# Destination tiles padded to groups of 32 edge records instead of blocks of 128: a list of superblock-and-tile units steers the sums

## The chip, the cores and the metric

The kernel runs on one core of one Trainium2 chip. The metric is the device time of one execution in microseconds (us). The core has five engines with their own instruction streams: PE (TensorE, matrix products), DVE (VectorE), ACT (ScalarE), POOL (GpSimd, which issues the indirect DMAs here) and SP (SyncE, which issues plain DMAs). They wait for each other on semaphores only.

## The reference

A graph layer over 3125 nodes of 256 channels, with 50,000 edges, in this form:

```python
xn = layernorm(x)
x = x + gnn(xn, src, dst, edge_weight) + mix(xn)
x = x + moe_ffn(layernorm(x))          # top 2 of 8 experts

def gnn(x, row, col, val, W, b):       # row = src, col = dst
    support = segment_sum(val[:, None] * x[col], row, num_segments=3125)
    return relu(concatenate([x, support], axis=1) @ W + b)
```

`mix` is a chain of pointwise convolutions with a batch norm, a linear attention inside groups of 32 channels and a residual map. All of it is in float32. The change concerns `support`: for every edge a row is fetched by `dst`, weighted and added to the row of `src`. The kernel fetches rows of the product with the second half of W (`y_d`), so that the sums land directly on the layer's output.

## The kernel before, in words

**Tiles and blocks.** The 3125 nodes are 25 tiles of 125 rows (`NT`, `T`). At run time the edges are sorted by the tile of their `src` into records of index, row within the tile and weight (three bf16 parts). The sort works in groups of 32 records (`GE`). Each tile's groups are padded up to whole blocks of 128 records (`nblk`, `bcum` of line 1122 on, with `EG` = 4 groups a block), so a block belongs to one tile. The list is as long as it can ever need to be: `EB` = 415 blocks.

**Work of a block.** POOL gathers 128 rows of 256 channels into a ring of 15 slots (lines 518 to 524). DVE compares the row numbers of 8 blocks at once with an iota (`hots`, line 1210). ACT scales one block's 0/1 matrix by the weights (`select`, line 874), up to 8 ahead. PE multiplies it with the gathered rows (`sum_edges`, line 641); a float32 product shows as two MATMUL records. Two blocks share a PSUM bank (`pair`, line 316), two banks alternate. DVE adds each block's 125 x 256 sum to its tile in `ACC` (`add_sums`, line 1233). Which tile that is comes out of a packed row: four 5-bit digits per loaded word (`digits`, line 1224). PE may be two banks, that is four blocks, ahead of DVE (`need(pe, g_acc, b - 2)`).

**Stages.** The order of every engine is written out by hand. After the sort come: the projection, 42 products of 500 columns (`project`, line 651) with 2 blocks each; the batch norm, with 18 blocks; the mixing stage, 28 segments of one tile each (`SEG`, line 697 on for PE, 1311 on for DVE), with 281 blocks dealt out in quarters of a segment (`mark`, `cut4`); a closing part with the last 32 blocks (`GT`) between 25 column operations of DVE and 25 squares of ACT, and then between 25 additions to `X`. Then the router, and a loop over 56 blocks of tokens for the experts.

**Within a segment** DVE does `shrink` and `key_sums`, a quarter of the additions, `inverses` (a reciprocal of 125 x 512, line 1292), a quarter, `values` and `queries`, a quarter, `products`, a quarter. PE does `channel_rows`, a quarter of the blocks, `channel_sums`, a quarter, `mix_transpose`, a quarter, `mix_out`, a quarter.

**Loads.** SP loads three experts' W2 (1 MB each) during the closing part, each behind a count of finished additions (line 420), and all of W1 once PE has done the last block.

## Time and profile before

| quantity | value |
|---|---|
| device time, three runs | 1198.22, 1188.03, 1197.9 us; median 1197.9 |
| profiled execution, span from first to last instruction | 1198.5 us |
| busy share of the span | PE 83%, weight loads 67%, DVE 63%, ACT 49%, POOL 54% |
| gathers | 415, the first at 155.83 us, the last at 702.0 us |
| mean granted clock of TensorE | 0.889 of full speed |
| HBM traffic | 86.44 MB read, 18.42 MB written |

The profile is of one execution. Its span, 1198.5 us, is all that the page gives of that execution's own time; it is 0.6 us above the median of the three runs. Busy time says how long an engine was at work, not whether somebody waited for it: for that one reads what ended the idle time before an instruction, and in the chain of waits which work was late.

### The profile page before, as it was taken

The page shows a single profiled execution, that of the slowest core. Times are in us where ns is not written, and L with a number is a line of the kernel's source. Part 1 is how long each engine was busy: PE and PEld are TensorE (multiplying, and loading weights), DVE is VectorE, ACT ScalarE, POOL GpSimd, SP SyncE. Part 2 cuts the span into 40 slices and gives each one's busy share as a digit, 9 for nine tenths or more (in the row PEclk, how much of TensorE's full clock was granted, in tenths as well). Part 3 has the DMA queues.
Part 4 walks back from the last instruction along what each step waited for, and adds up shares of the span by engine and source line. Part 5 has one row for each costly group of instructions (what it writes and reads, how often), then busy time and mean ns, then how long its engine had stood idle before and what let it go on. Part 6 is the DMA issues. An engine that isn't in the chain of part 4 may idle for free.

```text
span 1198.5 us, 20145 instructions
## 1 busy us (share of the span) xinstructions
PE 992.0 (83%) x5428; PEld 804.2 (67%) x5429; DVE 757.2 (63%) x1675; ACT 587.7 (49%) x1528; POOL 650.2 (54%) x620
## 2 busy tenths in 40 slices
PE   2779879985787777787777777499999999999995
PEld 1346545553566656666665457389999999999995
DVE  8999866653777777777877895634444444444441
ACT  0445445559766777766766733233333333333331
POOL 4393367777777777766767761214333344333332
PEclk8899989996878888888988765599999999999998
DMA  7012133333333333333333559352222222222221
GB/s 169 27 36 86 37 90 105 104 104 105 103 101 103 104 103 104 100 95 90 100 93 98 157 214 361 112 162 37 39 41 36 36 36 36 37 39 38 38 37 18
DMA packets 55071, 105.72 MB, mean 88 GB/s; under 512 B 15337, under 2 KB 37070, under 8 KB 52822
## 3 DMA queue, kind: packets, MB, share of 16 engines
q0 software_dynamic: 31312, 70.22, 23.8%
q1 hardware_dynamic: 23075, 33.81, 9.0%
q10 hardware_dynamic: 611, 0.87, 0.2%
q8 instruction: 28, 0.46, 0.2%
q14 instruction: 45, 0.37, 0.1%
HBM read 86.44 MB, written 18.42 MB: 87 GB/s over the span
## 4 chain that ended last, share of the span: by engine, by line
PE 54%; DVE 24%; issue 12%; DMA 3%; DVEq 3%; SPq 1%; ACT 1%; POOL 1%; ACTq 0%; POOLq 0%
PE ps L778 15%; PE ps L788 15%; PE ps L646 8%; DVE arena_c L1242 7%; PE ps L693 5%; PE ps L655 5%; DVE arena_a L1175 3%; DVE arena_a L1169 2%; DVE arena_c L1292 2%; DMA arena_c<-y_d,arena_e 1%; PE ps L724 1%; DVEq L1230 1%; PE ps L768 1%; SPq L450 1%; PE ps L735 1%
## 5 line engine op out<-in xcount | busy, mean ns | idle before, releaser
L523 POOL DMA_INDIRECT arena_c<-y_d,arena_e x415 | 407.9, 983 | 146.3 <-issue 87.4
L646 PE MATMUL ps<-arena_c,arena_e 128*125 128x256 f32 x830 | 257.7, 434 | 111.6 <-DVE arena_c L1242 97.0
L646 PEld LDWEIGHTS ps<-arena_c,arena_e 128*125 128x125 f32 x830 | 161.2, 213 | 190.1 <-issue 151.7
L1242 DVE TENSOR_TENSOR arena_c<-arena_c,ps 125x256 f32 x415 | 172.5, 416 | 100.3 <-PE ps L646 85.0
L555 POOL DMA_INDIRECT out<-node,bn x56 | 99.4, 1776 | 250.2 <-DVE node L1526 225.8
L879 ACT ACTIVATE arena_e<-arena_e 128x125 f32<-128x125 bf16 x415 | 190.6, 508 | 69.9 <-PE ps L646 57.4
L1002 ACT ACTIVATE arena_d<-ps,small 128x128 f32<-128x128 f32 x448 | 121.9, 383 | 181.0 <-PE ps L778 142.9
L788 PE MATMUL ps<-arena_c,arena_d 128*128 x896 | 204.0, 381 | 0.5 <-issue 0.5
L788 PEld LDWEIGHTS ps<-arena_c,arena_d 128*128 128x128 f32 x896 | 167.0, 191 | 21.4 <-issue 0.7
L778 PEld LDWEIGHTS ps<-node,arena_d 128*128 128x128 f32 x896 | 105.8, 194 | 2.6 <-DVE node L1518 1.2
L778 PE MATMUL ps<-node,arena_d 128*128 128x128 f32 x896 | 106.1, 277 | 0.8 <-DVE node L1518 0.8
L778 PEld LDWEIGHTS ps<-node,arena_e 128*128 128x128 f32 x896 | 104.4, 192 | 2.4 <-DVE node L1518 1.1
L778 PE MATMUL ps<-node,arena_e 128*128 128x128 f32 x896 | 104.7, 275 | 0.8 <-DVE node L1518 0.8
L1531 DVE TENSOR_SCALAR arena_e<-arena_e 128x256 f32<-128x256 f32 x56 | 23.1, 413 | 113.4 <-DMA arena_e<-z_d,bn 113.4
L1292 DVE RECIPROCAL arena_c<-arena_c 125x512 f32<-125x512 f32 x25 | 83.7, 3347 | 4.4 <-issue 4.4
L693 PE MATMUL ps<-arena_d 128*125 128x256 f32 x200 | 73.5, 534 | 0.0
L655 PE MATMUL ps<-arena_c,arena_d 128*128 128x500 f32 (+1 forms) x168 | 71.5, 549 | 2.3 <-DVEq L1208 2.3
L544 POOL DMA_INDIRECT arena_e<-z_d,bn x56 | 56.0, 1000 | 25.5 <-issue 12.8
L1013 ACT ACTIVATE node<-ps,bn 128x256 f32<-128x256 f32 x56 | 26.6, 475 | 86.0 <-PE ps L788 84.6
L1526 DVE SCALAR_TENSOR_TENSOR node<-arena_a,bn,node 128x256 f32<-128x256 f32 x56 | 27.1, 484 | 61.3 <-ACT node L1013 58.5
L693 PEld LDWEIGHTS ps<-arena_d 128*125 128x125 f32 x200 | 54.5, 272 | 13.1
L1518 DVE TENSOR_SCALAR node<-ps,small 128x128 f32<-128x128 f32 x112 | 40.8, 406 | 27.5 <-PE ps L768 25.9
(315 smaller groups left out, 1361.2 us busy)
## 6 DMA issues: line engine op xcount, KB each, us to landing
arena_c<-in_W SPq DMA_DIRECT2D x8, 1024.0 KB, 6.6
arena_a<-in_W SPq DMA_DIRECT2D x8, 1024.0 KB, 12.1
arena_c<-y_d,arena_e POOLq DMA_INDIRECT x415, 2.8
x<-in_x SPq DMA_DIRECT2D x5, 560.0 KB
z_d<-x SPq DMA_DIRECT2D x5, 560.0 KB
out<-x SPq DMA_DIRECT2D x5, 560.0 KB
y_d<-arena_c SPq DMA_DIRECT2D x15, 125.0 KB
y_d<-arena_a SPq DMA_DIRECT2D x10, 125.0 KB
```

The costliest lines, as they stand in the source:

```text
L523: pool.indirect_dma_start(ring[:, b % GR, :], None, io["y_d"], bass.IndirectOffsetOnAxis(gix[:, b:b + 1], 0)).then_inc(gth[b % GR], 16)
L544: pool.indirect_dma_start(xsb[b % 4], None, io["z_d"], bass.IndirectOffsetOnAxis(fetch[:, b:b + 1], 0)).then_inc(xs_in[b % 4], 16)
L555: pool.indirect_dma_start(io["out"], bass.IndirectOffsetOnAxis(home[:, b:b + 1], 0), ysb[b % 2], None, compute_op=ALU.add, oob_is_err=True ...
L646: nc.tensor.matmul(pair(b), sel[b % SR], ring[:, b % GR, :], start=True, stop=True).then_inc(g_mm, 1)
L655: mm = nc.tensor.matmul(ps[:, j, 0:w], wq[:, k, 128 * j:128 * j + 128], HT[:, k, i * TC:i * TC + w], start=(k == 0), stop=(k == 1))
L693: mm = nc.tensor.matmul(ps[0:T, 5, 0:C], oT[t % 2][:, k, :], wres[:, k, :], start=(k == 0), stop=(k == 3))
L778: mm = nc.tensor.matmul(psf[:, 1024 * s + 128 * j:1024 * s + 128 * j + 128], W1b[s][:, k, 128 * j:128 * j + 128], xeT[s][:, k, :], start=( ...
L788: mm = nc.tensor.matmul(out, gel[s][:, 128 * k:128 * k + 128], W2[:, ds(e, 1), k, :], start=(k == 0), stop=(k == 7))
L879: nc.scalar.activation(sel[b % SR], hot[b // 8 % 2][:, :, b % 8], ACT.Copy, scale=wcols[:, b:b + 1]).then_inc(selm, 1)
L1002: ins = nc.scalar.activation(gel[s % 2][:, 128 * j:128 * j + 128], psf[:, 1024 * (s % 2) + 128 * j:1024 * (s % 2) + 128 * j + 128], ACT.Ge ...
L1242: V.tensor_tensor(part, part, pair(b), ALU.add).then_inc(g_acc, 1)
L1292: V.reciprocal(rden, den[t % 2]).then_inc(v_at, 1)
```

## The change

Tiles are padded to groups of 32 only. Blocks of 128 records (`BG` = 4 groups) now follow each other without regard to tiles: `EB` = 397. Two blocks make a superblock of 256 records (`EG` = 8 groups, `SB` = 199). A unit is the part of one superblock that belongs to one tile; there are at most `EU` = 199 + 24 = 223. Each unit takes two products, one for each block of its superblock, summed in one PSUM bank, and one addition of DVE. Two selection matrices go with each unit (`EN` = 446); records of another tile get a row number outside 0 to 124 and so a zero column. The lists of units (tile, superblock, last unit of each superblock) are computed at run time by `unit_steps` and `unit_rows` on DVE with three small products on PE. PE reads the superblock from a packed row, three to a word. The ring has 16 slots. SP, which was idle then, waits for the two gathers of each superblock and raises `landed`, and waits for the superblock's last unit and raises `freed`, for which POOL waits. Stages: 42 units in the projection, 9 in the batch norm, 156 in the 28 segments, 16 in the closing part (6, 1, 6 and 3). The W2 loads of the closing part go to ACT's queue, between its squares.

```diff
-EB = (EC * T + NT * 127) // 128
+GM = (EC * T + NT * (GE - 1)) // GE
+EB = -(-GM // BG)
+SB = -(-GM // EG)
+EU = SB + NT - 1
+EN = 2 * EU
...
-        def pair(b):
-            return ps[0:T, 6 + b // 2 % 2, C * (b % 2):C * (b % 2) + C]
+        def unit_sums(u):
+            return ps[0:T, 6 + u % 2, 0:C]
...
-            for e in range(3):
-                sp.wait_ge(g_acc, EB - GT + 3 + 8 * e)
-                load_w2(e)
+            for s in range(SB):
+                d = s - (RS - RL)
+                if d >= 0:
+                    if d % 3 == 0:
+                        packed = sp.value_load(nrow[0:1, d // 3:d // 3 + 1], min_val=0, max_val=2 ** 24 - 1)
+                        for i in range(3):
+                            left[d + i] = (packed >> 8 * i) & 255
+                    sp.wait_ge(g_mm, sp.compute_val(left.pop(d) + 1))
+                    sp.sem_inc(freed, 1)
+                for b in range(2 * s, min(2 * s + 2, EB)):
+                    sp.wait_ge(gth[b % GR], 16 * (b // GR + 1))
+                sp.sem_inc(landed, 1)
...
             for b in range(EB):
-                need(pool, g_mm, b - GR + 1)
+                if b % 2 == 0:
+                    need(pool, freed, b // 2 - RS + 1)
...
-            def sum_edges(b):
-                pe.wait_ge(gth[b % GR], 16 * (b // GR + 1))
-                pe.wait_ge(selm, b + 1)
-                if b % 2 == 0:
-                    need(pe, g_acc, b - 2)
-                nc.tensor.matmul(pair(b), sel[b % SR], ring[:, b % GR, :], start=True, stop=True).then_inc(g_mm, 1)
+            def sum_edges(u):
+                if u % 3 == 0:
+                    packed = pe.value_load(srow[0:1, u // 3:u // 3 + 1], min_val=0, max_val=2 ** 24 - 1)
+                    for i in range(3):
+                        blocks[u + i] = pe.compute_val((packed >> 8 * i) & 255)
+                s = blocks.pop(u)
...
+                pe.wait_ge(landed, pe.compute_val(s + 1))
+                pe.wait_ge(selm, 2 * u + 2)
+                need(pe, g_acc, u - 1)
+                for j in range(2):
+                    mm = nc.tensor.matmul(unit_sums(u), sel[(2 * u + j) % SR], ring[:, ds(at + j, 1), :].rearrange("p a c -> p (a c)"),
+                                          start=(j == 0), stop=(j == 1))
+                mm.then_inc(g_mm, 1)
...
-                if b % 2 == 0:
-                    v.wait_ge(g_mm, min(b + 2, EB))
-                need(v, g_acc, b)
-                V.tensor_tensor(part, part, pair(b), ALU.add).then_inc(g_acc, 1)
-                digits(b + 1)
-                if b % 8 == 3:
-                    hots(b // 8 + 2)
+                v.wait_ge(g_mm, u + 1)
+                need(v, g_acc, u)
+                V.tensor_tensor(part, part, unit_sums(u), ALU.add).then_inc(g_acc, 1)
+                digits(u + 1)
+                if u % 4 == 1:
+                    hots(u // 4 + 2)
...
+                if t % 8 == 3:
+                    act.dma_start(W2[:, t // 8, :, :], io["W2"][t // 8]).then_inc(w2_in, 16)
```

On PE, at the start of the projection, before: `L655` is a projection product, `L646` a block's product, its waits on the instruction itself.

```order
L655 MATMUL ps<-arena_c,arena_d 128x500 [waits acc_ready,ld_w,y_ready,edge_records]
L655 MATMUL ps<-arena_c,arena_d 128x500
L646 MATMUL ps<-arena_c,arena_e 125x256 [waits selection_ready,gathered0]
L646 MATMUL ps<-arena_c,arena_e 125x256 [waits selection_ready,gathered1]
L655 MATMUL ps<-arena_c,arena_d 128x500 x2
L646 MATMUL ps<-arena_c,arena_e 125x256 [waits selection_ready,gathered2]
L646 MATMUL ps<-arena_c,arena_e 125x256 [waits selection_ready,gathered3]
```

The same place in the changed kernel, where `L706` is the projection product and `L685` to `L695` are one unit.

```order
L706 MATMUL ps<-arena_c,arena_d 128x500 [waits ld_w,edge_records]
L706 MATMUL ps<-arena_c,arena_d 128x500
L685 TENSOR_LOAD arena_e
L685 ISA x2
L687 REGISTER_ALU x5
L689 REGISTER_ALU
L689 ISA
L695 ISA [waits selection_ready,superblocks_landed]
L695 MATMUL ps<-arena_c,arena_e 125x256
L695 ISA
L695 MATMUL ps<-arena_c,arena_e 125x256
L706 MATMUL ps<-arena_c,arena_d 128x500 x2
```

Two blocks' products have become two products with four register and address instructions around them, twelve in every third unit, and the wait stands on an instruction of its own ahead of the first product.

On DVE, from one addition of a mixing segment to the next `shrink`, before: `L1242` adds a block, `L1228` and `L1230` unpack digits, `L1214` is `hots`, `L1280` `shrink`.

```order
L1242 TENSOR_TENSOR arena_c<-arena_c,ps 125x256 [waits g_acc]
L1228 TENSOR_LOAD arena_e
L1228 ISA x2
L1230 REGISTER_ALU x7
L1214 TENSOR_TENSOR arena_e<-arena_e,arena_d 128x1000 [waits selection_ready]
L1238 ISA
L1242 TENSOR_TENSOR arena_c<-arena_c,ps 125x256 [waits g_acc,g_mm]
L1238 ISA
L1242 TENSOR_TENSOR arena_c<-arena_c,ps 125x256 [waits g_acc]
L1280 TENSOR_SCALAR small<-small 125x1 [waits mix_root]
```

The same quarter in the changed kernel: `L1319` adds a unit, `L1306` and `L1308` unpack digits, `L1356` is `shrink`.

```order
L1319 TENSOR_TENSOR arena_c<-arena_c,ps 125x256 [waits g_acc,g_mm]
L1306 TENSOR_LOAD arena_e
L1306 ISA x2
L1308 REGISTER_ALU x7
L1316 ISA
L1319 TENSOR_TENSOR arena_c<-arena_c,ps 125x256 [waits g_acc,g_mm]
L1356 TENSOR_SCALAR small<-small 125x1 [waits mix_root]
```

Three additions have become two, each of two blocks. Over the stage it is 281 before and 156 now, and one unpacking goes to four units where it went to four blocks.

On SP, which had nothing here before, early in its loop over superblocks: `L440` loads a packed word, `L443` unpacks it.

```order
L443 REGISTER_ALU x2
L443 REGISTER_ALU [waits g_mm,gathered10,gathered11]
L443 REGISTER_ALU x2
L443 REGISTER_ALU [waits g_mm,gathered12,gathered13]
L443 REGISTER_ALU x2
L440 TENSOR_LOAD arena_e [waits g_mm,gathered14,gathered15]
L440 ISA x2
L443 REGISTER_ALU x2
```

Each wait names the last unit of an old superblock (`g_mm`) and the two gathers of a new one; the following register instructions carry the two signals.

## Rows read from the trace of the kernel before

**Rows 1.** The page: busy time by engine, and the gathers' and selections' groups
```profile
PE 992.0 (83%) x5428; PEld 804.2 (67%) x5429; DVE 757.2 (63%) x1675; ACT 587.7 (49%) x1528; POOL 650.2 (54%) x620
...
L523 POOL DMA_INDIRECT arena_c<-y_d,arena_e x415 | 407.9, 983 | 146.3 <-issue 87.4
...
L879 ACT ACTIVATE arena_e<-arena_e 128x125 f32<-128x125 bf16 x415 | 190.6, 508 | 69.9 <-PE ps L646 57.4
...
arena_c<-y_d,arena_e POOLq DMA_INDIRECT x415, 2.8
```

**Rows 2.** Stages: busy us and (x) count of PE, PEld, DVE, ACT, POOL; clock, DMA
```profile
165.00:265.00 100.00, 96.60 (x318) 57.56 (x318) 63.40 (x137) 53.73 (x119) 75.73 (x79) 1.00 0.36 104
265.00:296.00 31.00, 16.72 (x42) 8.75 (x40) 13.59 (x38) 25.94 (x26) 23.60 (x25) 0.76 0.36 105
296.00:669.00 373.00, 286.86 (x1314) 230.22 (x1314) 276.97 (x465) 255.56 (x611) 274.35 (x282) 0.86 0.34 100
669.00:710.00 41.00, 26.91 (x62) 15.63 (x62) 35.91 (x97) 23.55 (x79) 26.32 (x26) 0.64 0.51 164
800.00:1198.00 398.00, 385.12 (x2630) 362.09 (x2630) 166.12 (x470) 138.82 (x470) 148.25 (x106) 0.98 0.24 36
```

**Rows 3.** Timeline of POOL: start, duration; in brackets its idle time before
```profile
155.83 0.99 POOL L523 DMA_INDIRECT arena_c<-y_d,arena_e  x1 [7.10 <-DVE arena_e L1201]
...
159.90 3.82 POOL L523 DMA_INDIRECT arena_c<-y_d,arena_e  x1 [0.31 <-issue]
...
457.62 1.22 POOL L523 DMA_INDIRECT arena_c<-y_d,arena_e  x1 [0.30 <-PE ps L646]
...
497.44 0.94 POOL L523 DMA_INDIRECT arena_c<-y_d,arena_e  x1 [0.85 <-PE ps L646]
...
702.00 0.95 POOL L523 DMA_INDIRECT arena_c<-y_d,arena_e  x1 [0.30 <-issue]
```

**Rows 4.** The gathers in 155 to 497.4 us: busy us and (x) count
```profile
155.00:497.40 342.40, 260.63 (x264) 0.88 0.35 102
```

**Rows 5.** Groups of the mixing stage, 296 to 669 us
```profile
L523 POOL DMA_INDIRECT arena_c<-y_d,arena_e x282 | 275.7, 978 | 99.0 <-issue 60.9 <-PE ps L646 38.0
L646 PE MATMUL ps<-arena_c,arena_e 128*125 128x256 f32 x564 | 170.0, 424 | 85.7 <-DVE arena_c L1242 82.4 <-ACT arena_e L879 2.8
...
L1242 DVE TENSOR_TENSOR arena_c<-arena_c,ps 125x256 f32 x280 | 115.9, 414 | 65.4 <-PE ps L646 54.8 <-DVE arena_c L1242 4.0
```

**Rows 6.** Timeline of DVE in one mixing segment
```profile
457.34 0.68 DVE L1214 TENSOR_TENSOR arena_e<-arena_e,arena_d 128x1000 bf16<-128x1000 bf16 x1 [0.61 <-issue]
...
460.99 3.35 DVE L1292 RECIPROCAL arena_c<-arena_c 125x512 f32<-125x512 f32 x1 [0.75 <-issue]
464.26 1.34 DVE L1242 TENSOR_TENSOR arena_c<-arena_c,ps 125x256 f32 x3
```

**Rows 7.** Timeline of PE: projection, its end, mixing, expert loop
```profile
186.64 1.84 PE L655 MATMUL ps<-arena_c,arena_d 128*128 128x500 f32 x4
188.31 1.03 PE L646 MATMUL ps<-arena_c,arena_e 128*125 128x256 f32 x4
...
270.64 2.23 PE L646 MATMUL ps<-arena_c,arena_e 128*125 128x256 f32 x4 [0.85 <-DMA arena_c<-y_d,arena_e]
...
296.19 1.64 PE L671 MATMUL ps<-small,arena_a 128*125 128x128 f32 x6 [6.16 <-ACT arena_a L898]
...
465.23 1.19 PE L646 MATMUL ps<-arena_c,arena_e 128*125 128x256 f32 x2 [3.30 <-DVE arena_c L1242]
...
1004.34 0.38 PE L768 MATMUL ps<-small,arena_e 128*128 128x128 f32 x2
1004.56 3.62 PE L788 MATMUL ps<-arena_c,arena_d 128*128 x16
```

**Rows 8.** The chain of waits: DVE's queue just before an addition
```profile
441.62 0.07 DVEq L1238
```

**Rows 9.** Timeline of SP's queue: the issues of W1
```profile
709.50 4.08 SPq L428 DMA_DIRECT2D arena_a<-in_W  x8
```

275 lines of the change are left out of this document (163 added, 112 removed).

## The prediction

> **What bounds the kernel now.** I read the page first. It shows no engine busy throughout, PE 83% and POOL 54% [rows 1], so the share of an average says little and the span has to be cut into stages [rows 2]. The expert loop from 800 us on is PE alone, busy 385 of 398 us, and the change does not reach it. What the change touches lies between the first gather at 155.83 us and the last addition of an edge block, at 710 us.
>
> Next, POOL's timeline [rows 3]. A gather takes 0.94 to 0.95 us with 0.30 between two; 264 have started before the one at 497.44 [rows 4], so the pitch up to there is (497.44 - 155.83) / 264 = 1.294 us. Its wait of 0.85 us for PE is the first that exceeds the usual gap: until then POOL never had to wait for a free slot, after it once in each segment. So POOL paces nothing from the start of the mixing stage on; it only catches up. Had it never waited, 415 gathers at 1.294 us would be through at 693, and the last one starts at 702.0.
>
> In the projection PE is busy 96.6 of 100 us [rows 2]: four records of the projection take 1.67 us from start to start (186.64 to 188.31), and the four of two blocks their 1.03 less an overlap as large as the projection's, 1.84 - 1.67 = 0.17, so 0.86, a period of 2.53 us [rows 7]. Two gathers at 1.294 are 2.59. The two limits are equal there, and at the end of the stage, where the projection products are narrow, PE waits for gathers (0.85 us before 270.64).
>
> In the mixing stage (296 to 669 us, 28 segments, 13.3 us each) nobody is full: PE 287, DVE 277, ACT 256, POOL 274 of 373 us [rows 2]. The groups say who waits for whom [rows 5]: PE waits 82.4 us for additions, and DVE 54.8 us for products. That is a handover chain: DVE is in its reciprocal for 3.35 us, PE has its two banks full and idles 3.30 us (before 465.23), then DVE does three additions in a row [rows 6, 7]. The clock of 0.86 in this stage is the other mark of it, since it falls after such gaps. DVE's own load is higher than its busy time: unpacking digits leaves it idle for 0.61 to 0.75 us a time [rows 6], and each addition has an address instruction of 0.07 us [rows 8], with which I count as much again for the gap around it.
>
> **The sort's end and the start of the projection.** `unit_steps` takes the place of the old block list and is about as long. The weight parts now go through 16 products of 228 columns where 16 transposes of 104 stood, then DVE's four conversions on 456 columns instead of 416. None of this is in my rows; the bounds are 0 and 5 us, and I take 2. The first gather does not wait for it. PE's first products wait for gathers anyway: the fourth, at 159.90, took 3.82 us [rows 3], beside DVE's long bias addition, and this stays. Effect on the end: nothing, because of the gathers; 2 to 5 us if the cover were gone.
>
> **Projection.** 42 units take as long on PE as 84 blocks (four records of 256 columns each), but need 42 x 397 / 223 = 75 gathers instead of 84. PE then no longer waits for them. From the third product, at about 166.5 us (the fourth gather has landed by then), 34 wide periods of 2.53 and 6 narrow ones (125 columns in place of 500, a quarter of 1.67, and 0.86) make 94, so the batch norm starts at about 262 instead of 270. The batch norm is ACT's six activations with 18 selections between them, and keeps its length. The mixing stage starts at 296 - 8 = 288. By then POOL can have done (288 - 155.8) / 1.294 = 102 gathers, and the ring allows 51 x 1.78 + 16 = 107: no stall.
>
> **Mixing, DVE.** A segment has 5.57 units instead of 10.04 blocks. Additions: 4.47 fewer, at 0.414 us [rows 5] and 0.14 for the address [rows 8], 2.5 us. Unpacking: 1.39 instead of 2.51 times, at 0.75, 0.8 us. `hots`: 0.14 more at 0.68, 0.1 us. Net 3.2 us less of 13.3.
>
> **Mixing, PE.** 11.14 products instead of 10.04, that is 2.2 more records at 170.0 / 564 = 0.30 us [rows 5], 0.7 us more; 19 us over the stage. PE's load goes from 287 to 306 us, 10.9 a segment. DVE's was 277 plus what is neither busy nor a wait for products, 373 - 277 - 54.8 = 41, so 318; less 28 x 3.2 = 90 it is 228, 8.1 a segment. Before, the period was 13.3 over a higher load of 318 / 28 = 11.4: a loss of 17% to the handover. The same loss on 10.9 gives 12.7; with no loss it is 10.9.
>
> **Mixing, the register instructions of PE.** A unit has four of them, every third unit a load and seven more. DVE's rows bound the price: 0.75 us for a load with what unpacks it, 0.14 for an address [rows 6, 8]. That is at most 0.75 / 3 + 3 x 0.14 = 0.67 us a unit. From below it is nothing: in the expert loop every product has an address instruction too and 16 records run in 3.62 us right behind L768, without a gap behind a load either [rows 7]. I take 0, as that is the same engine, and the instructions stand behind the previous product and ahead of the wait. The Trainium skill ("Advanced Engine Details and Errata", section Sequencer Loop) says of control instructions that other engine instructions can be read and queued while they execute; PE's expert rows agree, DVE's gaps of 0.61 to 0.75 us do not.
>
> **Mixing, the gathers as a floor.** 368 of 397 gathers must have landed by the end of the stage: 155.8 + 368 x 1.294 + 3.7 = 635.7, which from 288 is 12.4 us a segment. (3.7 us is 0.95 and the 2.8 to landing of [rows 1].) So neither limit gives the full gain of 3.2 us. I take 12.6 us: 28 x 12.6 = 353, the stage ends at 641, and 20 of its 373 us are gone. The gathers' pitch stays: the one at 457.62 takes 1.22 us, 0.27 more, beside a `hots` from 457.34 on, and of those there are 56 instead of 52 [rows 3, 6]; the additions removed read PSUM. The Trainium skill ("SBUF — State Buffer", Who interferes with whom) infers that a `tensor_tensor` leaves descriptor generation alone. By that rule the pitch would be 0.95 + 0.30 = 1.25, 397 gathers 17 us shorter, and the floor would not bind; the row speaks against it.
>
> **ACT** gets 31 more selections of 0.46 us (190.6 / 415) [rows 1], 14 us over 500, and in the mixing stage it idles 117 of 373 us [rows 2]: hidden. Its three W2 issues stand in its loop of squares, which is as long as DVE's there; SP's eight issues of 1 MB take 4.08 us [rows 9], 0.51 each, so 1.5 in sum, and 0 if DVE is later there. **SP's relay** puts a hop between a gather and its product. Even at DVE's 0.75 us it is shorter than the 2.59 of two gathers, so it delays each but slows none, and POOL may be 3 superblocks ahead of SP. I take 0; the other end is 0.75 us once for every stretch in which PE waits for gathers, some 5 in all.
>
> **Closing part**, 41 us before. DVE has 13 additions instead of 25 between its 50 operations: in the first loop ACT's squares hold the time, in the second 6 x 0.41 = 2.4 us go. The rest after the loops is 3 units instead of 7 blocks, 1.5 us. With ACT's 1.5 added back, 38.5 us. The last gather lands at 155.8 + 397 x 1.294 + 3.7 = 673, so it does not hold this part.
>
> **Sum.** 288 + 353 + 38.5 = 679.5 instead of 710, 30.5 us less. Against the profiled span that is 1168.0, and 0.6 less against the median. I say 1168.
>
> **The rivals.**
> - *The handover stays as slow as it is.* PE waits in the reciprocal because two banks are full, and they still are two: PE still gets four products ahead. If each segment keeps 13.3 us, what remains is 8 + 2.5: 1188. For it: the 3.30 us gap is the reciprocal's, not the additions'. Against it: 2.5 us of additions less, and a turn is now one addition.
> - *The gathers alone bind.* With a chain under 12 us the end is 673 + about 3 of last products: 34 us less, 1164. For it speaks DVE's load of 8.1 us; against it the closing part, which follows its own 38.
> - *Slower: PE's register instructions stand on its path.* If a load waits for the array, or the queue is empty after each wait, up to 0.67 us a unit is added: 156 x 0.67 = 105 in the mixing stage, 28 in the projection, 11 in the end. PE's load in mixing would be 306 + 105 = 411; with 20 of waits 431, so 1198.5 + 58 + 28 + 11 - 10.5 = 1285. At half that price it is 378 + waits as before, 1198.5 + 5 + 14 + 5 - 10.5 = 1212. It turns to a loss from some 0.2 us a unit: 306 + 31 = 337, with a tenth of handover 371, and 8 more in the projection. For it: DVE does show such gaps, and in the segments PE, unlike in the expert loop, starts from an empty queue after each wait. Against it: the expert rows.
> - *The change doesn't do what it says:* the counts follow from the constants (397, 446, 223); only a gather count of 415 in the trace would show it. No chance worth a figure.
>
> **How the numbers follow.** The forecast 0.52 (1157 to 1180), the gathers alone 0.10, the unchanged handover 0.25, the register path 0.13. One per cent, 12 us, is about what a measurement of this kernel can tell from no change; the three runs already spread over 10. Faster by over 1% (below 1186): 0.52 + 0.10 + 0.11 of the third case = 0.73. Slower: the register case with 0.12. Within 1%: 0.15. The range 1155 to 1197 holds the first three cases and the unknowns of 5 us at the sort's end; it leaves out the register case and a little on the fast side.
>
> **What would show it.** Right: no PE wait for gathers before 262 us; the mixing stage 345 to 360 us; PE's waits for additions well below 82 us; POOL's waits for a free slot few. Wrong: idle "issue" time of PE ahead of a unit's first product, PE's records of a unit spread over more than 0.9 us in the projection, or segments of 13.3 us with PE idle beside the reciprocal as before.

## The result and the profile after

The changed kernel takes 1161.8 us (median of 4 runs, 1160.4 to 1163.6), the kernel before 1198.1 beside it (4 runs, 1188.0 to 1198.5): a ratio of 0.970, 95% interval 0.966 to 0.975. The forecast was 1168.0 with a range of 1155 to 1197. The profiled execution has a span of 1158.4 us instead of 1198.5, so 40.1 us are to be found in the trace. They stand in two places: 30.1 us up to the last addition of an edge unit, which ends at 679.9 instead of 710.0 us, and 10.0 us behind it (1158.4 - 679.9 = 478.5 instead of 488.5), where the change touches nothing.

The page of the changed kernel, engines, the chain by engine and line, and the groups of the gathers, the units' products, the selections and the additions:

```profile
PE 967.4 (84%) x5493; PEld 789.4 (68%) x5494; DVE 686.8 (59%) x1501; ACT 599.7 (52%) x1559; POOL 635.0 (55%) x603
...
PE 40%; POOL 24%; DVE 12%; DMA 12%; issue 10%; SPq 2%; ACT 0%; DVEq 0%; POOLq 0%; ACTq 0%
...
L550 POOL DMA_INDIRECT arena_c<-y_d,arena_e x397 | 395.6, 996 | 128.2 <-issue 105.7
L695 PE MATMUL ps<-arena_c,arena_e 128*125 x892 | 258.1, 421 | 97.2 <-SPq L447 71.6
...
L929 ACT ACTIVATE arena_e<-arena_e 128x125 f32<-128x125 bf16 x446 | 202.3, 510 | 67.5 <-PE ps L695 53.1
...
L1319 DVE TENSOR_TENSOR arena_c<-arena_c,ps 125x256 f32 x223 | 92.2, 414 | 167.6 <-PE ps L695 164.8
```

The counts are those of the change (397, 446, 223). The two last columns carry the news. TensorE's wait ahead of an edge product now ends with L447, SyncE's relay, which passes on that a superblock's gathers have landed; before, it ended with L1242, the additions [rows 5]. VectorE waits 164.8 us for products: it has become the one with time to spare. And POOL stands in the chain that ended last with 24% of the span.

The stages of the changed kernel by the windows (busy us and count of PE, PEld, DVE, ACT, POOL; granted clock, DMA share, GB/s), cut where [rows 2] cut the kernel before:

```profile
165.00:265.00 100.00, 100.00 (x341) 62.14 (x339) 50.52 (x104) 58.56 (x128) 76.54 (x78) 1.00 0.34 103
265.00:291.00 26.00, 12.83 (x31) 7.83 (x30) 6.91 (x21) 23.92 (x23) 19.60 (x22) 0.63 0.34 103
291.00:643.40 352.40, 278.16 (x1374) 225.02 (x1374) 229.68 (x346) 268.31 (x641) 269.68 (x272) 0.94 0.34 102
643.40:680.00 36.60, 22.48 (x65) 15.02 (x65) 29.85 (x82) 23.08 (x80) 24.34 (x23) 0.81 0.51 170
760.00:1158.00 398.00, 385.16 (x2630) 362.15 (x2630) 164.97 (x469) 138.41 (x470) 147.83 (x106) 0.98 0.23 36
```

The projection has no wait of TensorE's left (100.00 of 100 us). Mixing starts at 291 instead of 296 and takes 352.4 instead of 373 us; the closing part 36.6 instead of 41. The expert loop is the same to 0.04 us.

POOL's timeline, from the first gather to the last:

```profile
158.04 0.99 POOL L550 DMA_INDIRECT arena_c<-y_d,arena_e  x1 [7.53 <-DVE arena_e L1275]
159.33 0.95 POOL L550 DMA_INDIRECT arena_c<-y_d,arena_e  x1 [0.30 <-issue]
...
164.38 3.23 POOL L550 DMA_INDIRECT arena_c<-y_d,arena_e  x1 [0.30 <-issue]
...
460.96 1.41 POOL L550 DMA_INDIRECT arena_c<-y_d,arena_e  x1 [0.30 <-issue]
...
673.30 0.95 POOL L550 DMA_INDIRECT arena_c<-y_d,arena_e  x1 [0.30 <-issue]
```

Between these 397 gathers no idle time is over 0.36 us, so POOL never waits for a free slot: (673.30 - 158.04) / 396 = 1.301 us each, from one end to the other. That is the picture of the rival "the gathers alone bind", not of the forecast, in which gathers and handover were about level. The last gather lands 2.8 us after its start, at 676.1, and the last addition ends at 679.9. What lies between is TensorE's, as its timeline and a window of it show:

```profile
669.21 1.13 PE L695 MATMUL ps<-arena_c,arena_e 128*125 x4 [1.67 <-SPq L447]
671.84 7.59 PE L695 MATMUL ps<-arena_c,arena_e 128*125 x20 [1.50 <-SPq L447]
```

```profile
672.00:678.00 6.00, 6.00 (x15) 4.53 (x16) 4.61 (x12) 0.93 (x2) 1.95 (x2) 0.50 0.21 66
```

At 671.84 TensorE has waited for a gather for the last time. It then works off the last five units in one stretch, most of it at a granted clock of 0.50, to which it has fallen in that wait. So the gathers set the pace up to there, and the last 8 us are products, most of them at the low clock.

The reciprocals of VectorE, one to a mixing segment, show where one limit gives way to the other:

```profile
302.24 3.35 DVE L1368 RECIPROCAL arena_c<-arena_c 125x512 f32<-125x512 f32 x1
...
311.87 3.34 DVE L1368 RECIPROCAL arena_c<-arena_c 125x512 f32<-125x512 f32 x1
...
321.33 3.35 DVE L1368 RECIPROCAL arena_c<-arena_c 125x512 f32<-125x512 f32 x1 [0.74 <-ACT arena_c L975]
...
332.29 3.35 DVE L1368 RECIPROCAL arena_c<-arena_c 125x512 f32<-125x512 f32 x1
```

The first segments take 9.6, 9.5 and 11.0 us. They find some 11 gathered blocks in the ring: at 290.8 us 102 gathers have started and 51 units have used 51 x 1.78 = 91. Once these are used up, from 332.29 on to the 25th reciprocal at 605.70, 21 of them take 13.0 us on average. A segment of 5.57 units needs 5.57 x 397 / 223 = 9.9 gathers, and 9.9 x 1.301 is 12.9. What looked like a stage of even 12.6 us segments, as forecast, is a short fast piece and a long one at the gathers' pace.

The 10 us behind the last addition are in the token products and transposes of the router. Their windows, first of the kernel before (30 us), then of the changed one (18.7 us):

```profile
710.00:740.00 30.00, 29.54 (x150) 28.99 (x150) 17.40 (x62) 10.87 (x27) 13.08 (x16) 0.50 1.00 372
```

```profile
679.90:698.60 18.70, 17.43 (x150) 15.74 (x150) 17.43 (x61) 10.87 (x27) 13.10 (x16) 1.00 0.97 393
```

It is the same work, 150 instructions on TensorE. Before, it runs at a granted clock of 0.50 (1.2 GHz) from end to end, although TensorE is busy 29.54 of 30 us; after, at 1.00 (2.4 GHz). The difference is 11.3 us, of which 10.0 are left at the end of the span.

### The profile page after: what moved, and what is told of

The parts are those of the page before. It is cut to its first block, busy times and chain, and to the rows that moved or that the text cites. A ratio compares the mean times of both kernels' runs of the same rounds, so it can differ in the third digit from the quotient of the medians.

```text
span 1158.4 us, 21890 instructions
## 1 busy us (share of the span) xinstructions
PE 967.4 (84%) x5493; PEld 789.4 (68%) x5494; DVE 686.8 (59%) x1501; ACT 599.7 (52%) x1559; POOL 635.0 (55%) x603
## 4 chain that ended last, share of the span: by engine, by line
PE 40%; POOL 24%; DVE 12%; DMA 12%; issue 10%; SPq 2%; ACT 0%; DVEq 0%; POOLq 0%; ACTq 0%
POOL arena_c L550 24%; PE ps L828 17%; PE ps L838 17%; DMA arena_c<-y_d,arena_e 10%; DVE arena_a L1248 3%; DVE arena_a L1242 2%; SPq L440 1%; PE ps L638 1%; PE ps L818 1%; PE ps L615 1%; PE ps L774 1%; DMA z_d<-gates 1%; DVE small L1109 1%; PE ps L695 1%; DVE arena_a L1245 1%
## 5 line engine op out<-in xcount | busy, mean ns | idle before, releaser
L550 POOL DMA_INDIRECT arena_c<-y_d,arena_e x397 | 395.6, 996 | 128.2 <-issue 105.7
L695 PE MATMUL ps<-arena_c,arena_e 128*125 x892 | 258.1, 421 | 97.2 <-SPq L447 71.6
L695 PEld LDWEIGHTS ps<-arena_c,arena_e 128*125 128x125 f32 x892 | 169.5, 203 | 168.6 <-issue 148.3
L929 ACT ACTIVATE arena_e<-arena_e 128x125 f32<-128x125 bf16 x446 | 202.3, 510 | 67.5 <-PE ps L695 53.1
L1319 DVE TENSOR_TENSOR arena_c<-arena_c,ps 125x256 f32 x223 | 92.2, 414 | 167.6 <-PE ps L695 164.8
L706 PE MATMUL ps<-arena_c,arena_d 128*128 128x500 f32 (+1 forms) x168 | 71.1, 546 | 2.7 <-DVEq L1287 2.7
L571 POOL DMA_INDIRECT arena_e<-z_d,bn x56 | 55.8, 996 | 26.5 <-issue 13.4
L537 POOL DMA_INDIRECT rec_d<-arena_e x20 | 26.4, 1318 | 45.9 <-ACT arena_e L898 45.1
L615 PE MATMUL ps<-node,arena_c 128*125 128x512 f32 x100 | 50.3, 628 | 0.0
## 6 DMA issues: line engine op xcount, KB each, us to landing
arena_a<-in_W SPq DMA_DIRECT2D x8, 1024.0 KB, 12.4
```

The lines of the kernel that those rows point to most:

```text
L550: pool.indirect_dma_start(ring[:, b % GR, :], None, io["y_d"], bass.IndirectOffsetOnAxis(gix[:, at:at + 1], 0)).then_inc(gth[b % GR], 16)
L571: pool.indirect_dma_start(xsb[b % 4], None, io["z_d"], bass.IndirectOffsetOnAxis(fetch[:, b:b + 1], 0)).then_inc(xs_in[b % 4], 16)
L615: mm = nc.tensor.matmul(ps[0:T, 5 + t % 3, :], HT[:, k, T * t:T * t + T], gnn2[:, k, :], start=(k == 0), stop=(k == 1))
L695: mm = nc.tensor.matmul(unit_sums(u), sel[(2 * u + j) % SR], ring[:, ds(at + j, 1), :].rearrange("p a c -> p (a c)"), start=(j == 0), stop ...
L706: mm = nc.tensor.matmul(ps[:, j, 0:w], wq[:, k, 128 * j:128 * j + 128], HT[:, k, i * TC:i * TC + w], start=(k == 0), stop=(k == 1))
L929: nc.scalar.activation(sel[b % SR], hot[b // 8 % 2][:, :, b % 8], ACT.Copy, scale=wcols[:, b:b + 1]).then_inc(selm, 1)
```

## The experiments

All ran beside runs of the kernel before on the same chip. "Mixing segment" is the mean distance of the 25 reciprocals, "last addition" its end in the profiled execution; for the kernel before these are 13.78 us and 710.0, for the changed one 12.64 and 679.9.

**Half of the gathers, in either kernel.** Changed kernel:

```diff
-            for b in range(EB):
-                if b % 2 == 0:
-                    need(pool, freed, b // 2 - RS + 1)
+            for b in range(0, EB, 2):
+                need(pool, freed, b // 2 - RS + 1)
...
-                for b in range(2 * s, min(2 * s + 2, EB)):
+                for b in range(2 * s, 2 * s + 1):
...
-                    ... ring[:, ds(at + j, 1), :] ...
+                    ... ring[:, ds(at, 1), :] ...
```

> The changed kernel with 199 gathers in place of 397: the second gather of each superblock is left out, and both products of a unit read the first one's 128 rows (so half of the edge records contribute nothing, and the others stand in for them). Products, selections and additions keep their number. Theory (in the changed kernel the gathers alone bind the mixing stage, at 1.301 us each without a gap from 158 to 673 us): the segments fall from 12.6 us to what the first of the changed kernel's took while the ring was still full, 9.5 to 11 us, say 10.3; 28 segments make 64 us, so about 1098 us, within 1085 to 1110. Rival (the handover between TensorE and VectorE binds, and the gathers only run beside it): 1162 within 10 us, with segments of 12.6 us as before.

Measured: 1089.3 us (1083.8 to 1093.4), ratio 0.910 (0.903 to 0.917). The segment is 10.13 us, the last addition at 605.8.

The kernel before got the same cut, the product of an odd block reading the slot of the even one:

> The kernel before with every second gather left out (208 in place of 415), the product of an odd block reading the rows of the even one before it. Theory (before the change the handover of additions bound the mixing stage and the gathers only trailed it): segments stay near 13.3 us; POOL's own stretch and the narrow products at the end of the projection give 0 to 10 us, so 1188 to 1198, I say 1193. Rival (before, too, the gathers were what bound): 28 segments go to about 11 us, 60 us less, 1138.

Measured: 1195.9 us (10 runs, 1194.8 to 1198.2), ratio 1.000 (0.997 to 1.003). The segment is 13.74 us, against 13.78 with all gathers. The mixing stage began 5 us earlier, and so did the last addition end, at 705.0.

The same cut takes 73 us from the changed kernel and 2 from the one before. So the gathers bind the one and did not bind the other. The groups say it as plainly. Of the changed kernel with half of its gathers, 300 to 560 us, the window, then additions, gathers, products:

```profile
300.00:560.00 260.00, 233.31 (x1303) 199.23 (x1303) 221.42 (x333) 251.31 (x611) 128.57 (x131) 1.00 0.23 67
...
L1318 DVE TENSOR_TENSOR arena_c<-arena_c,ps 125x256 f32 x146 | 59.6, 408 | 22.2 <-PE ps L694 20.4
L549 POOL DMA_INDIRECT arena_c<-y_d,arena_e x131 | 129.4, 988 | 133.9 <-SPq L444 120.8 <-issue 13.1
L694 PE MATMUL ps<-arena_c,arena_e 128*125 x581 | 147.7, 385 | 26.7 <-DVE arena_c L1318 14.4 <-ACT arena_e L928 11.6 <-SPq L447 0.4
```

And of the kernel before with half of its gathers, the products from 300 to 600 us:

```profile
L647 PE MATMUL ps<-arena_c,arena_e 128*125 128x256 f32 x439 | 134.6, 428 | 72.1 <-DVE arena_c L1243 69.3 <-ACT arena_e L880 2.4
```

In the second, TensorE's 69.3 us of waits for additions stand just as with all the gathers (66.4 us in the same window of the kernel before). In the first, the wait for gathers is 0.4 us, and the next limit comes into sight: ScalarE is busy 251 of 260 us. With its 11 selections and the conversions of a segment it would hold a segment at 251.3 / 260 x 10.13 = 9.8 us, however fast the rest were.

**The register instructions.** As the first, and the superblock of unit u is the constant `u * SB // EU` on TensorE's and SyncE's queues, with no load, unpacking or address instruction:

```diff
-                if u % 3 == 0:
-                    packed = pe.value_load(srow[0:1, u // 3:u // 3 + 1], ...)
...
+                s = u * SB // EU
+                at = s % RS * 2
```

> As the changed kernel with half of its gathers, and besides the list of superblocks is not read: unit u takes superblock u*199//223, a constant, on TensorE's and SyncE's queues, so neither has a load, an unpacking or an address instruction for a unit; the records added are not those of the unit. With the gathers out of the way TensorE's instructions are on the path. Theory (the register instructions of TensorE cost nothing): the same time as with half of the gathers alone, within 5 us. Rival (they stand on TensorE's path at 0.2 us or more a unit): 156 units of mixing at 0.2 to 0.67 us, 30 to 105 us faster than with half of the gathers alone.

Measured: 1081.7 us (1078.6 to 1089.1), against 1089.3 with the gathers alone halved; the intervals of the two ratios (0.899 to 0.913 and 0.903 to 0.917) overlap. The segment is 10.03 instead of 10.13 us, so leaving these instructions out shows in mixing with 0.1 / 5.57 = 0.02 us a unit, 3 us over the stage. ScalarE's 9.8 us stand close under either segment and could hide a little more. The projection is the stricter place, as TensorE has no gap there with half of the gathers. First two periods of the kernel before (no register instructions), then of the changed kernel with them, both with half of the gathers:

```profile
181.88 1.84 PE L656 MATMUL ps<-arena_c,arena_d 128*128 128x500 f32 x4
...
184.42 1.84 PE L656 MATMUL ps<-arena_c,arena_d 128*128 128x500 f32 x4
```

```profile
180.87 1.84 PE L705 MATMUL ps<-arena_c,arena_d 128*128 128x500 f32 x4
...
183.41 1.84 PE L705 MATMUL ps<-arena_c,arena_d 128*128 128x500 f32 x4
```

A period is 2.54 us in both: where TensorE has no gap, these instructions add nothing to the period. The rest of the 12.7 us between the two profiled spans is mostly the router's clock again: behind its last addition the first has 485.5 us left with the token products at clock 0.54, the second 477.0 us with clock 1.00. The rival of 0.2 us a unit or more has fallen.

**Additions twice, in either kernel.** The addition is done once more, into scratch space:

```diff
+                V.tensor_tensor(scratch, part, unit_sums(u), ALU.add)
                 V.tensor_tensor(part, part, unit_sums(u), ALU.add).then_inc(g_acc, 1)
```

> The changed kernel with each unit's addition done twice on VectorE, the first time into scratch space nobody reads: 223 more instructions of 0.41 us. Theory (gathers bind the mixing stage with 2.3 us a segment of slack on VectorE's chain, which is just 5.57 additions of 0.41 us): mixing costs 0 to 10 us more, the closing part 13 additions or 5 us: about 1170, within 1163 to 1180. Rival (the chain through VectorE binds all along): 169 additions after the projection at 0.41 us, 69 us more, 1231.

Measured: 1168.3 us (1162.9 to 1173.5), ratio 0.979 (0.972 to 0.985), so 6.5 us more than the changed kernel; the segment is 12.49 us, not longer than without (12.64).

> The kernel before with each block's addition done twice on VectorE, the first time into scratch space, as it was done to the changed kernel (which it cost 6.5 us): 415 more instructions of 0.41 us, 331 of them after the projection. Theory (before, the chain through VectorE binds): nearly all of the 280 in the mixing stage and of the 50 behind it show, 3.5 us a segment, about 100 us more, 1300, within 1260 to 1330. Rival (VectorE is not on the path before either): up to 20 us more, 1218.

Measured: 1286.6 us (1286.1 to 1287.0), ratio 1.077 (1.070 to 1.085). The segment is 16.72 us, 2.94 more for 10.04 more additions of 0.41 us (4.1): some of it is absorbed, but 88.5 us reach the end. The chain through VectorE's additions was the limit before and no longer is.

**One cut at a time.** In the kernel before, either only the change's number of gathers, or only about its number of additions, or both:

```diff
             for b in range(EB):
+                if b % 23 == 22:
+                    continue
```

```diff
-                nc.tensor.matmul(pair(b), sel[b % SR], ring[:, b % GR, :], start=True, stop=True)...
+                nc.tensor.matmul(pair(b - b % 2), sel[b % SR], ring[:, b % GR, :], start=(b % 2 == 0),
+                                 stop=(b % 2 == 1 or b == EB - 1))...
...
                 if b % 2 == 0:
...
-                V.tensor_tensor(part, part, pair(b), ALU.add).then_inc(g_acc, 1)
+                    V.tensor_tensor(part, part, pair(b), ALU.add).then_inc(g_acc, 2)
```

> The kernel before with the change's number of gathers and nothing else of it: 18 of the 415 gathers, every 23rd, are left out (the product of such a block reads what its slot held before), 415 products and 415 additions stay. Theory (before, the handover of additions binds, and even half of the gathers gave nothing): 0 to 8 us faster, say 1195. Rival (the change's gain is its 18 fewer gathers): 18 x 1.3 = 23 us faster, 1175.

Measured: 1190.2 us (10 runs, 1183.2 to 1196.5), ratio 0.996 (0.991 to 1.0003); segment 13.78, last addition 705.2. The 4.8 us come before the mixing stage, where TensorE waits less for gathers; in mixing nothing is gained.

> The kernel before with the change's cut in additions and nothing else of it: two blocks are summed in one bank and added once, to the tile of the even block (which leaves the tile borders out), so 208 additions instead of 415; 415 gathers, 415 products and 415 selections stay. Theory (with the additions cut the gathers bind at once: 415 at 1.30 us from 155.8 us land at 699, the last addition comes at about 702 instead of 710): 8 us faster, 1190, within 1183 to 1195. Rival (the additions were the whole cost, the gathers are only near): some 28 us faster, 1170.

Measured: 1188.2 us (10 runs, 1185.3 to 1190.3), ratio 0.993 (0.990 to 0.997); segment 12.95, last addition 699.0. The products' group of this kernel, 300 to 600 us, shows what took the place of the additions at once:

```profile
L646 PE MATMUL ps<-arena_c,arena_e 128*125 128x256 f32 x471 | 153.1, 421 | 62.7 <-DMA arena_c<-y_d,arena_e 59.4 <-ACT arena_e L880 0.7
```

68.2 us of waits have become 62.7, with another name at their end. 10.04 gathers at 1.30 us are 13.05 us, and that is the segment.

> The kernel before with both cuts: 208 additions and 397 gathers, but with its static blocks, no list of units and no register instructions on TensorE, and 415 products in place of 446. Leaves the tile borders and 18 gathers out. Theory (the change is worth what its two cuts are worth together, and everything else in it costs nothing): 397 gathers at 1.30 us land at 675 and the last addition comes at 677 to 680: 30 us faster, 1167, within 1156 to 1172. Rival (the units' products, the list or SyncE's relay cost something in the changed kernel): at least 8 us below the changed kernel's 1162, 1154 or less.

Measured: 1161.4 us (1155.2 to 1167.9), ratio 0.971 (0.963 to 0.979), the changed kernel's 1161.8; segment 12.35, last addition 680.0 (the changed kernel's 679.9). Cutting gathers alone brings 8 us by the medians, cutting additions alone 10, both 37; by the last additions, which leave the router's clock out, it is 4.8, 11.0 and 30.0. (The 8 us by the medians are not clear of none, the interval reaching 1.0003.) That is the answer to what the change is worth and why: it cuts two limits that stood 11 us apart, and either cut alone runs into the other.

Whether everything else in the change (the list, 31 products more, SyncE's relay) is free, the equal last additions do not settle. POOL's last gather in the kernel with both cuts:

```profile
676.04 0.95 POOL L525 DMA_INDIRECT arena_c<-y_d,arena_e  x1 [0.30 <-PE ps L648]
```

It starts 2.7 us later than the changed kernel's, at 673.30, but the last addition comes 3.9 us behind it and not 6.6. And of the four runs of this kernel two, at 1155.2 and 1157.2 us, lie below all four of the changed kernel; the profiled one took 1167.9, with 486.1 us behind its last addition instead of 478.5. A price of 8 us or more, as the rival had it, does not show; one of up to some 5 us is not excluded.

**The router's clock, and three more.** Four kernels ran on a third chip, on which the kernel before takes 1291.2 us (7 runs, 1287.8 to 1293.0) instead of 1198. Comparisons within this group stand; the sums in the expectations, made from the other chips' times, don't. What is different there shows in the waits of the changed kernel with the added products (engine, line, what ended the wait: us, times, longest):

```profile
DVE arena_c L1321 <- remote: 150.5, 39, 8.2
ACT arena_e L931 <- remote: 60.3, 24, 7.7
ACT arena_a L937 <- remote: 21.3, 3, 10.0
```

Waits of up to 10 us here, and up to 13.4 in the other three kernels, end with "remote", a name that no wait of the profiles on the other chips carries. In one such stretch three engines stand nearly still while POOL goes on, as the window of the same kernel shows:

```profile
182.80:191.80 9.00, 0.70 (x2) 0.00 (x0) 0.52 (x2) 0.00 (x0) 5.46 (x6) 0.67 0.34 103
```

It begins with VectorE, idle for 12.64 us ahead of an addition without any wait that the profile shows. The cause was not found. In this kernel POOL waits 114 us for free slots and in the next two 119 and 95, so on this chip the gathers don't bind, and what an experiment does to the gathers can be read in the gathers' own durations, but not in the time.

```diff
             for b in range(EB - GT, EB):
                 sum_edges(b)
+                for _ in range(2):
+                    nc.tensor.matmul(ps[0:T, 4, 0:C], ident[:, 0:T], wres[:, 0, :], start=True, stop=True)
```

> The kernel before with two products more behind each of the last 32 blocks on TensorE (125x256, into a bank that nobody reads, 0.3 us each at the full clock), 64 in all, which work to no end but keep the array from idling in the closing part. The runs of the kernel before fall into two groups, 1188 to 1192 us at a mean granted clock of 0.904 and 1196 to 1201 at 0.892, and in its profile the 75 token products and transposes behind the last addition run at clock 0.50 for 28 us, in the changed kernel's at 1.00 for 16. Theory (what differs is the clock at which TensorE enters that stretch, which it then keeps): all runs near 1188, the stretch at clock 1.00, 10 us faster than the median of before. Rival (the clock there has another cause): 1198 as before, or more by the products' own time, 5 to 15 us.

Measured: 1278.5 us (1274.9 to 1280.6), ratio 0.991 (0.989 to 0.993), which is 12.7 us less than the kernel before on the same chip, with 64 products more. The windows of this kernel at the end of its closing part and in the token products:

```profile
780.00:790.00 10.00, 10.00 (x48) 8.63 (x48) 8.75 (x23) 2.11 (x4) 0.00 (x0) 1.00 0.31 107
...
795.60:814.00 18.40, 17.19 (x151) 15.55 (x150) 17.25 (x61) 10.91 (x27) 12.95 (x16) 1.00 0.99 401
```

TensorE goes into the token products at clock 1.00, and they take 18.4 us, about as in the changed kernel. On this chip no profile of the kernel before exists, so that it has them at 0.50 here too is taken from its time, not shown; and the changed kernel has them at 1.00 in all three of its variants on this chip, two of which have no additional products.

The theory's second half, that TensorE keeps the clock at which it enters, does not hold. The kernel before enters the token products at 0.50 and stays there, also with its additions doubled or cut. Seven profiles, the changed kernel's and this one's among them, stay at 1.00 from end to end. But in four others (half of the gathers in either kernel, 397 gathers, both cuts) TensorE enters at 1.00 and falls to 0.50 after 1 to 3 us. The changed kernel with half of its gathers, from its last addition on:

```profile
605.80:608.40 2.60, 2.45 (x18) 2.02 (x19) 2.57 (x7) 0.94 (x3) 2.42 (x3) 0.97 0.78 211
608.40:634.00 25.60, 25.60 (x134) 25.52 (x133) 14.66 (x54) 9.48 (x24) 10.66 (x14) 0.50 1.02 390
```

Ahead of it, from 596.0 to 605.8, it had been busy 7.22 of 9.8 us at a clock of 0.90; in the variant without register instructions it was busy 7.43 of the last 9.6 us at 0.85 and stayed at 1.00 behind them. So the 10 us are the clock's in the token products and not the change's doing, but what decides on that clock stays open.

The same in the changed kernel, three products behind each unit (`range(EU - GT, EU)`, `range(3)`):

> The changed kernel with three products more behind each of its last 16 units on TensorE, 48 in all, as in the kernel before. Theory: the changed kernel already enters the token products at the full clock in the runs seen (1160 to 1164 us), so within 3 us of 1162; if some of its runs were to fall into a slower group at 1172, this one has none. Rival (the additional products delay the last units, each by up to 0.9 us at the full clock): 5 to 15 us slower, 1172.

Measured: 1266.2 us (1263.3 to 1272.2), ratio 0.980 (0.978 to 0.983). The changed kernel itself was not run on this chip, so whether 48 more products help or harm it is not settled. The token products run at the full clock, 19.1 us from the last addition to their end. With products added to both kernels the last additions end at 795.3 and 791.2 us: in these two profiles, with the stretches of unknown cause in both, the change is worth about 4 us up to there and not 30.

```diff
-                V.tensor_tensor(grouped(vr), grouped(rden), grouped(ab[t % 2])[:, :, 64:96], ALU.mult)...
+                V.tensor_tensor(grouped(vr)[:, :, 0:2], grouped(rden)[:, :, 0:2], grouped(ab[t % 2])[:, :, 64:66], ALU.mult)...
```

and so for `queries` and `products`.

> The changed kernel with VectorE's three products of a node tile (values, queries and products, 125x512 in fp32 from SBUF, 0.69 us each) cut to 2 of 32 columns of each group, 125x32, so 15/16 of the attention's output is left out; nothing else changes. Of the 397 gathers those that take more than 0.95 us do so beside VectorE operations with two SBUF sources, 19.8 us in sum, about 9 to 10 of it beside these three. Theory (such an operation stretches the gather it meets, and the gathers bind): 9 to 10 us faster, 1152. Rival (the stretch has another cause, and VectorE's 1.6 us less a segment changes nothing, as its chain doesn't bind): 1162.

Measured: 1275.2 us (1270.9 to 1280.3), ratio 0.989 (0.986 to 0.993). The time says nothing on the theory, the gathers not binding; the gathers' group answers instead, below.

```diff
-        rowb = cut(UP, BF16)
+        rowb = cut(2 * UP)
```

> The changed kernel with the row numbers that VectorE compares with (rowb) in fp32 instead of bf16; the comparison then has one fp32 source, and 128x1000 elements will take longer than 0.67 us, I expect 1.1. Theory (any operation with two SBUF sources stretches a gather, for as long as it runs, whatever its type, since the fp32 products of 125x512 do it too): the 56 comparisons stretch as much or more, 0 to 6 us slower, 1164. Rival (what stretches is the fast bf16 form alone): the 5 us or so beside the comparisons go, 1157.

Measured: 1272.1 us (1267.6 to 1280.5), ratio 0.988 (0.984 to 0.992); again the gathers' group answers. The gathers' groups of the pages of these three kernels, first with the added products (whose VectorE work is that of the changed kernel), then with the three products of a node tile thinned out, then with fp32 row numbers:

```profile
L550 POOL DMA_INDIRECT arena_c<-y_d,arena_e x397 | 392.7, 989 | 224.5 <-SPq L444 114.2
```

```profile
L550 POOL DMA_INDIRECT arena_c<-y_d,arena_e x397 | 387.1, 975 | 228.8 <-SPq L444 119.3
```

```profile
L550 POOL DMA_INDIRECT arena_c<-y_d,arena_e x397 | 406.5, 1024 | 209.0 <-issue 103.5
```

The comparisons themselves went from 674 to 1194 ns. This is their row in the third kernel:

```profile
L1293 DVE TENSOR_TENSOR arena_e<-arena_e,arena_d 128x1000 bf16<-128x1000 f32 x56 | 66.8, 1194 | 4.3 <-ACT arena_e L929 2.3 <-issue 1.8 <-DVE arena_e L1285 0.2
```

So 397 gathers take 5.6 us less where the three products are nearly gone, and 13.8 us more where the comparisons run in fp32 and 0.52 us longer each (56 x 0.52 = 29 us). The 13.8 us are clear: it is not the fast bf16 form that stretches a gather, and the longer operation stretches it more. The 5.6 us, where 9 to 10 were claimed, are weaker. Taken over all gathers the stretch was 16 to 20 us in three profiles with the same operations of this kind, and only the share beside the three products, which went from 9 to 2 us, puts the fall where it was sought. And not each meeting counts: of the changed kernel's 397 gathers 56 take over 1.02 us, all beside a VectorE operation with two SBUF sources, while 53 others that share over 0.3 us with such an operation keep their 0.95 us.

## Why the prediction came out as it did

The time was inside the range, 6 us below the forecast. Its steps, one by one:

- *What bounds before: a handover between TensorE and VectorE, with POOL only trailing.* Shown right, twice: half of the gathers change nothing (1.000), twice the additions cost 88.5 us.
- *The end of the sort hides, "the first gather does not wait for it".* Wrong. The first gather starts at 158.04 instead of 155.83 [rows 3]; in the seven profiles with the old list it starts at 155.8 to 157.3, in the seven with the new one at 158.0 to 160.1. It waits for VectorE's index conversion, and that for TensorE's transposes of the sorted records, first of the kernel before, then of the changed one:

```profile
153.87 1.90 PE L633 MATMUL ps<-arena_c,arena_e 104*128 104x104 bf16 x20 [7.78 <-DMA arena_e<-rec_d]
```

```profile
155.72 0.50 PE L668 MATMUL ps<-arena_c,arena_e 100*128 100x100 bf16 x4 [7.55 <-DMA arena_e<-rec_d]
```

  They start 1.85 us later because the sort ends as much later: VectorE begins its last chunk at 141.59 us, before at 139.74. `unit_steps`, early in the sort, was taken to be "about as long" as the old list. Up to the next chunk it takes 3.2 us (73.96 to 77.17), the old list 1.5 (74.75 to 76.25), and a wait of 1.06 us for TensorE comes later. The bias addition of 3.36 us, which stands ahead of the conversion and ends at 156.7, half a us after the transposes, makes up the other 0.4. As far as the gathers bind, such a delay goes on to the end; no run shows it alone. The term was looked up against TensorE's needs only, not POOL's.
- *Projection: 8 us less.* 5.4 came (mixing starts at 290.8, not 288). The end of the projection was right: the period of 2.53 us held (2.54 in the trace), no product waited for a gather, and the batch norm's products begin at 262.3, forecast 262. (166.5 + 94 is 260.5; the 2 us that were to hide at the sort's end make it 262.) What it was compared with was not. The 270 us are the row before 270.64 [rows 7], a block of the batch norm; ScalarE's first activation there starts at 272.64 before and at 267.29 in the changed kernel, 5.35 us earlier:

```profile
272.64 2.99 ACT L898 ACTIVATE arena_a<-arena_a,bn 128x3125 f32<-128x3125 f32 x1 [0.86 <-DVE bn L1274]
```

```profile
267.29 2.99 ACT L948 ACTIVATE arena_a<-arena_a,bn 128x3125 f32<-128x3125 f32 x1 [0.86 <-DVE bn L1350]
```
- *Mixing: 12.6 us a segment, 353 us in all.* 12.64 and 352.6, from the wrong mechanism. I put TensorE's load at 10.9 us a segment and added the old loss of 17%. With the gathers out of the way the chain runs at 10.1 us. The load was sized too high because 287 us of busy time before held records at a clock of 0.86; at 1.00 the same work with 11% more products is 233 of 260 us, 9.1 us a segment. The floor of the gathers was worked out as 12.4 us and real at 12.6; it was the forecast's other leg and carries it alone. (Its landing term of 3.7 us counts 0.95 us twice, as the 2.8 us run from a gather's start; that is 0.03 us a segment.) I chose 12.6 between that floor and a chain of 12.7 that was sized wrong, so the closeness is partly luck. The rival "the gathers alone bind", to which I gave 0.10 at 1164 us, is what happened.
- *The handover stays as slow as it is (0.25).* Fell: TensorE's waits for additions in the mixing stage went from 82.4 us [rows 5] to 6.7. The group of the products there:

```profile
L695 PE MATMUL ps<-arena_c,arena_e 128*125 x624 | 177.6, 414 | 73.8 <-SPq L447 59.6 <-DVE arena_c L1319 6.7 <-ACT arena_e L929 5.9
```

- *Register instructions on TensorE cost nothing (0.13 for the contrary).* 0.02 us a unit in mixing, nothing in the projection. The Trainium skill ("Advanced Engine Details and Errata", section Sequencer Loop), by which engine instructions can be read and queued while control instructions execute, agrees with this measurement.
- *SyncE's relay: 0; selections on ScalarE: hidden.* Nothing contradicts either here: the kernel with both cuts has no relay and 31 selections fewer and the same last addition, with the reservation of up to 5 us made above. But ScalarE would be the next limit: with the gathers halved it is busy 9.8 of the 10.1 us of a segment.
- *W2 issues on ScalarE: 1.5 us.* They take 0.33 to 0.36 us each, 1.0 in sum.
- *Closing part: 38.5 us, and the last gather "does not hold this part".* 36.5 us came, and gathers do hold it: TensorE waits 11.2 us for them there, up to 671.84.
- *The sum up to the last addition: 679.5.* 679.9. The 0.4 us are luck: mixing began 2.8 us later than forecast, and the closing part was 2 us shorter.
- *Not in the forecast: 10 us of clock in the router.* I took everything behind the last addition as fixed. It is not: it has two lengths, 477 to 480 us and 485 to 491 in all profiled executions, by TensorE's clock in the token products. The kernel before has the long one in the profile; its 13 runs beside the first experiments fall into 1188 to 1192 us at a mean granted clock of 0.903 to 0.905 (5 runs) and 1196 to 1201 at 0.889 to 0.896 (8 runs). The four runs of the changed kernel lie within 3.2 us. So of the 36 us between the medians some 30 are the change's own, as the last additions show, and the rest is that the clock happened to stay up in its token products. That is not bound to hold: with each addition doubled, two of the four runs were 8 to 11 us longer than the shortest.

## What to carry to other kernels

Where two engines wait for each other and a third only trails, work out the trailing one's own pace first: it is the floor under everything that speeds up the other two, and here it stood 11 us under a chain that the change lowered by far more. The cheapest test is to halve each candidate's work in both kernels: a ratio of 1.000 before and 0.910 against 0.970 after settled in one step what busy shares left open. And busy time recorded at the lower TensorE clock is no load: recompute it at the full clock before adding a loss to it.

## What the runs showed of the hardware

- *TensorE can be busy 98% of 30 us and stay at 1.2 GHz.* 150 small instructions (128x48 products, 125x125 transposes) took 29.54 us at a granted clock of 0.50 throughout, in another execution 17.43 at 1.00. Entering them at 1.00 was not enough: in four profiles the clock fell to 0.50 within 3 us and stayed, in one of them with TensorE busy 25.60 of 25.60 us. The Trainium skill ("TensorE: Matmul & The Clock Gate", section Part 1: The HAM clock gate) has the engine go up to 2.4 GHz once it has been busy; these stretches speak against it for such work.
- *A gather of 128 rows costs POOL 0.95 us and 0.30 us to the next, 1.25 in sum, and VectorE can make it longer.* On average it was 1.301. Of the 397 gathers of the changed kernel, those over 0.95 us are 19.8 us longer in sum, beside VectorE operations with two SBUF sources, fp32 or bf16 alike; the two experiments above moved the gathers' busy time by -5.6 and +13.8 us. The Trainium skill ("SBUF — State Buffer", Who interferes with whom) says that such an instruction contends with a GpSimd instruction that reads SBUF, which these rows bear out, and infers that a `tensor_tensor` leaves descriptor generation alone. For an indirect gather these rows don't bear that out; whether the reading of its index or the generation is held up they don't tell.
- *Two chips ran the kernel before in 1198 us, a third in 1291*, with stretches such as one of 9 us in which three engines did next to nothing, for a cause that stayed open. What binds shifts with it (POOL waited for slots there), so kernels to be compared belong on one chip.
